# A three-layer graph network on one core: two neighbouring key columns stored side by side, and fetched with one gather for two

## The reference

```python
src = jnp.concatenate([edge_index[0], loops]); dst = jnp.concatenate([edge_index[1], loops])
deg = segment_sum(ones_like(dst), dst, num_segments=n)
dinv = where(deg > 0, rsqrt(deg), 0.0)
norm_edge = dinv[src] * dinv[dst]
for W, b in ((W1, b1), (W2, b2), (W3, b3)):
    h = h @ W
    h = relu(segment_sum(h[src] * norm_edge[:, None], dst) + b)
out = layernorm(x + h)
```

## Time and profile before

| | us |
|---|---|
| three runs | 2489.03, 2490.22, 2491.07 |
| median | 2490.22 |
| the profiled execution | 2488.2 |
| its span | 2486.4 |
| PE busy | 2271.8 (91%) |
| POOL busy | 1753.4 (71%) |
| DVE busy | 1027.0 (41%) |
| ACT busy | 521.7 (21%) |

### The profile page before, as it was taken

How to read it: one execution, slowest core, us unless ns; L and a number is a source line. 1 busy time by engine, 2 the same in 40 slices (tenths; PEclk the granted TensorE clock), 3 DMA queues, 4 the chain that set the end, 5 groups by cost and what they waited for, 6 DMA issues and landing times.

```text
span 2486.4 us, 42327 instructions
## 1 busy us (share of the span) xinstructions
PE 2271.8 (91%) x13351; PEld 1562.8 (63%) x13352; DVE 1027.0 (41%) x1307; ACT 521.7 (21%) x1322; POOL 1753.4 (71%) x1837
## 2 busy tenths in 40 slices
PE   6977799898999998999999999999988799999998
PEld 6855577676777773444444444444444688888887
DVE  8877333233333313444444444444422233333332
ACT  6611223222222312222222222222211000000000
POOL 5177777777777756777777777777776776767674
PEclk9788999999999999999999999999999899999999
DMA  6335666666666656888888888888887888888784
GB/s 215 119 118 184 222 203 206 201 198 205 192 209 190 208 170 204 253 272 268 267 264 264 263 267 264 264 268 258 275 260 236 261 257 249 252 248 255 245 247 140
DMA packets 231550, 568.24 MB, mean 229 GB/s; under 512 B 39868, under 2 KB 95795, under 8 KB 231475
## 3 DMA queue, kind: packets, MB, share of 16 engines
q0 software_dynamic: 126752, 399.62, 54.6%
q1 hardware_dynamic: 88371, 126.81, 14.5%
q10 hardware_dynamic: 16352, 40.77, 4.9%
HBM read 476.69 MB, written 90.36 MB: 228 GB/s over the span
## 4 chain that ended last, share of the span: by engine, by line
PE 55%; POOL 16%; issue 13%; DMA 7%; POOLq 4%; DVE 3%; ACT 0%; ACTq 0%; DVEq 0%; SPq 0%
POOL rows L671 16%; PE ps_acc L1511 9%; PE ps_h L1600 8%; PE ps_T L1600 7%; PE ps_o L1567 6%; DMA rows<-table,idx 5%; PE ps_d L1612 5%; PE ps_acc L1515 5%; PE ps_d L1515 4%; PE ps_h L1555 3%; PE ps_d L1511 3%; POOLq L680 3%; PE ps_d L1469 2%; DMA rows<-table_parts,idx 1%; PE ps_e L1588 1%
## 5 line engine op out<-in xcount | busy, mean ns | idle before, releaser
L671 POOL DMA_INDIRECT rows<-table,idx x912 | 870.0, 954 | 300.9 <-issue 264.7
L671 POOL DMA_INDIRECT rows<-table_parts,idx x884 | 837.1, 947 | 324.0 <-issue 268.2
L892 DVE SCALAR_TENSOR_TENSOR sel<-ps_e,firsts,dstT 128x1152 f32<-128x1152 f32 (+1 forms) x222 | 314.7, 1418 | 684.9 <-PE ps_acc L1511 253.9
L1515 PE MATMUL ps_acc<-rows,sel 128*128 128x512 f32 (+2 forms) x1122 | 489.8, 568 | 82.8 <-DMA rows<-table,idx 55.5
L1515 PE MATMUL ps_d<-rows,sel 128*128 128x512 f32 (+1 forms) x850 | 413.3, 616 | 41.3 <-DMA rows<-table,idx 41.2
L1511 PE MATMUL ps_acc<-rows,sel 128*128 128x256 bf16 (+1 forms) x2196 | 360.1, 280 | 50.5 <-DMA rows<-table_parts,idx 21.7
L1515 PEld LDWEIGHTS ps_acc<-rows,sel 128*128 128x128 f32 x1122 | 209.2, 202 | 250.0 <-issue 149.3
L1511 PEld LDWEIGHTS ps_acc<-rows,sel 128*128 128x128 bf16 x2196 | 217.9, 100 | 93.9 <-issue 37.8
L1515 PEld LDWEIGHTS ps_d<-rows,sel 128*128 128x128 f32 x850 | 152.8, 195 | 196.4 <-issue 119.2
L1567 PE MATMUL ps_o<-w,hT 128*128 128x512 f32 (+1 forms) x784 | 269.2, 486 | 1.2 <-ACT hT L1272 1.2
L1612 PE MATMUL ps_d<-parts,made_tiles 128*128 128x256 bf16 x1470 | 229.2, 272 | 0.5 <-issue 0.4
(11 more groups left out here) (190 smaller groups left out, 1902.8 us busy)
## 6 DMA issues: line engine op xcount, KB each, us to landing
built<-made_tiles SPq DMA_DIRECT2D x72, 384.0 KB
made_tiles<-built ACTq DMA_DIRECT2D x72, 384.0 KB
rows<-table,idx POOLq DMA_INDIRECT x912
rows<-table_parts,idx POOLq DMA_INDIRECT x884
table<-made SPq DMA_DIRECT2D x49, 256.0 KB
acc<-table SPq DMA_DIRECT2D x49, 256.0 KB
built<-made_tiles SPq DMA_DIRECT2D x24, 416.0 KB
made_tiles<-built ACTq DMA_DIRECT2D x24, 416.0 KB
```

The lines of the kernel that those rows point to most:

```text
L671: pool.indirect_dma_start(out=to, out_offset=None, in_=its[0:nodes, :], in_offset=bass.IndirectOffsetOnAxis(ap=idx[:, of, k:k + 1], axis=0 ...
L892: v.scalar_tensor_tensor(to[:, k:k + FRONT, :], numbers.unsqueeze(1).broadcast_to([P, FRONT, P]), firsts[:, bass.ds(t, 1)], dstT[:, bass.d ...
L1515: return mm(to[:, 0:w], sel[:, k, :], rows_of[phase][:, k, 0:w] if first is None else first, start=start, stop=stop)
```

## The change

In DRAM, `keys` becomes twice as wide: row c holds column c in its first 128 words, and column c + 1 in the second 128. SP stores the first halves as before, and the second halves with two further DMAs, both read from the same `raw_src`. Column c + 1 of partition q is partition q + 1 of the same block, so one store goes from partitions 1 to 127 of SBUF into the rows of q = 0 to 126; for q = 127 the neighbour is partition 0 of the next block, and that is the other store, 6 rows. The very last row's second half is not written. POOL waits for all three and fetches both columns of a chunk with one gather of 1 KB rows, six in place of twelve. `key_rows` keeps one row number for each chunk, and one of DVE's small instructions goes.

```diff
--- before.py
+++ after.py
@@ -118,7 +118,7 @@
 
 
 
-        keys = nc.dram_tensor("keys", (COLS, P), I32).ap()
+        keys = nc.dram_tensor("keys", (COLS, 2 * P), I32).ap()
         built = nc.dram_tensor("built", (DENSE * P, T * P), BF16).ap()
 
         raw = sb("raw", [P, 3, RA, P], I32)
@@ -207,7 +207,7 @@
         fill = sb("fill", [P, CHUNKS])
         fill_i = sb("fill_i", [P, CHUNKS], I32)
         over = sb("over", [P, CHUNKS])
-        key_rows = sb("key_rows", [P, 2, CHUNKS], I32)
+        key_rows = sb("key_rows", [P, CHUNKS], I32)
         bits = sb("bits", [P, len(SHIFTS), CHUNKS], I32)
         root = sb("root", [P, T])
         dinv = sb("dinv", [P, T])
@@ -467,7 +467,10 @@
             sp.wait_ge(place_out, 16)
             sp.dma_start(src_wide, places.rearrange("(a k) p -> a k p", a=1).broadcast_to([P, SLOTS, P])).then_inc(wide_in, 16)
             sp.wait_ge(keys_made, 1)
-            sp.dma_start(keys.rearrange("(a q) p -> q a p", q=P), raw_src).then_inc(keys_out, 16)
+            columns = keys.rearrange("(a q) p -> q a p", q=P)
+            sp.dma_start(columns[:, :, 0:P], raw_src).then_inc(keys_out, 16)
+            sp.dma_start(columns[0:P - 1, :, P:2 * P], raw_src[1:P, :, :]).then_inc(keys_out, 16)
+            sp.dma_start(columns[P - 1:P, 0:RA - 1, P:2 * P], raw_src[0:1, 1:RA, :]).then_inc(keys_out, 16)
             for g in range(XSTEPS):
                 by, nth_of = X_BY[g]
                 sp.wait_ge(x_scaled[by], nth_of)
@@ -701,14 +704,13 @@
                     else:
                         gather_if(need, phase, k, of, k, in_parts)
 
-            pool.wait_ge(keys_out, 16)
+            pool.wait_ge(keys_out, 16 * 3)
             pool.wait_ge(counts_in, 1)
             pool.wait_ge(key_rows_done, 1)
             for c in range(CHUNKS):
-                for side in range(2):
-                    pool.indirect_dma_start(
-                        out=kw[:, c, side * P:(side + 1) * P], out_offset=None, in_=keys[:, :],
-                        in_offset=bass.IndirectOffsetOnAxis(ap=key_rows[:, side, c:c + 1], axis=0)).then_inc(kw_in, 16)
+                pool.indirect_dma_start(
+                    out=kw[:, c, :], out_offset=None, in_=keys[:, :],
+                    in_offset=bass.IndirectOffsetOnAxis(ap=key_rows[:, c:c + 1], axis=0)).then_inc(kw_in, 16)
 
             def one_window():
                 for phase in range(3):
@@ -858,8 +860,7 @@
             v_.wait_ge(firsts_done, 1)
             step(v.tensor_copy(first_f[:, :, :], ps_acc[:, 0:2 * CHUNKS].rearrange("p (i c) -> p i c", i=2)))
             step(v.tensor_copy(first_i[:, :], first_f[:, 0, :]))
-            step(v.tensor_scalar(key_rows[:, 0, :], first_i[:, :], 7, None, ALU.arith_shift_right))
-            step(v.tensor_scalar(key_rows[:, 1, :], key_rows[:, 0, :], 1, None, ALU.add))
+            step(v.tensor_scalar(key_rows[:, :], first_i[:, :], 7, None, ALU.arith_shift_right))
             v_.wait_ge(next_in, 16 * 3)
             v.tensor_scalar(firsts[:, :], few[:, 0:T + 1], float(P), None, ALU.mult)
             step(v.tensor_copy(ends[:, :], raw_next[:, :, P - 2]))
@@ -1027,7 +1028,7 @@
 
             def shift_words():
 
-                v_.wait_ge(kw_in, 16 * 2 * CHUNKS)
+                v_.wait_ge(kw_in, 16 * CHUNKS)
                 for i, far in enumerate(SHIFTS):
                     n = P + far - 1
                     step(v.copy_predicated(kw[:, :, 0:n], bits[:, i, :].unsqueeze(2).broadcast_to([P, CHUNKS, n]),
```

## The result

| us | before | changed |
|---|---|---|
| median of 6 runs each | 2491.72 | 2505.29 |
| lowest to highest | 2489.03 to 2494.51 | 2501.90 to 2511.07 |
| the profiled execution | 2488.2 | 2504.32 |
| its span | 2486.4 | 2502.5 |
| mean granted clock of the profiled execution | 0.965 | 0.956 |

The ratio of the two is 1.0055, with a 95% interval of 1.0045 to 1.0065: by the medians the changed kernel is 13.6 us slower. The forecast was 2507.2, range 2500 to 2517.

What follows compares the result with a forecast made beforehand. POOL's full gather queue was taken to carry any delay of its first table gather to the end. The 127-row store on one engine delays the table, +17.0 us on 2488.2 gives 2505.2, plus 2.0 to the median: 2507.2, range 2500 to 2517.

Steps and rivals of the forecast that it cites:

- The store on one engine: Second keys' store, 127 x 7 rows: all rows go to one DMA engine of 16 and take 24.2 us.
- Its part of the table behind it: The slow engine's share of the seven table stores, 19.7 us, plus 1.4 for its part of the key gathers.
- Table landed at 145.7: `table0_out` complete at 145.7 us in place of 120.3, including 0.3 for the landing.
- The first table gather 1.8 us behind the landing, so +17.0: POOL's first table gather at 147.5 us, 17.0 later than 130.50.
- DVE +19.7: DVE's copy starts at 145.8 us, 19.7 late, and with it the splits, first sum and PE's opening of window 1.
- Rival C: DVE's splits set the pace of windows 1 to 3, 2.7 us not won back: 2509.9; within the forecast's 0.78.
- From then on everything is as late as POOL: After PE's waits for rows spend 2.7 us, everything downstream stays 17.0 us late.
- A: The 127-row store spreads over engines, table lands by 123.8, only 3.4 us of POOL's queue gained: 2486.8; chance 0.12.
- B: The lone engine is slower, 54 ns per 512-byte row, 48.5 us in place of 24.2: 2531.5; chance 0.04.
- D's second form: Table lands fully before the rest of the keys, so POOL's key gathers delay its table gathers: +23, 2513; chance 0.04.

Runs made afterwards that it cites:

- row counts: The kernel before, with eight extra stores of 128 to 112 partitions at its end, one after the other; 2565.13 us in one execution.
- padded kernel: The changed kernel with one more row in `keys`, so both halves are stored with 128 partitions; 2491.46 us, ratio 0.9995 to before.
- gathers-alone kernel: The kernel before without the six gathers of the column behind and without added stores; 2491.62 us, ratio 0.9996.
- slow store twice: The changed kernel with a second 127-row store in SP's queue, ahead of the table's stores; 2522.20 us, ratio 1.0125 to before.
- stores alone: The kernel before, twelve gathers kept, plus a 127-row and a 6-row store to DRAM that nobody reads; 2505.84 us, ratio 1.0059.
- slow store behind the table: The changed kernel with both added stores moved behind the table's seven stores in SP's queue; 2507.18 us, ratio 1.0063 to before.
- 126 rows and 1: The changed kernel with its 127-row store cut into one of 126 rows and one of 1; 2491.28 us, ratio 1.0004 to before.
- the one from POOL: The changed kernel with its two added stores issued by POOL on its own queue, not by SP; 2513.65 us, ratio 1.0082 to before.

## Why the prediction was right, and where its sizes were off

**The store on one engine** (forecast 24.2 us): it is. The share was 0.06 to 0.08 for 20 us, and the row counts show the rule at eight numbers. The term measured 21.5, since the lone engine moved 21.2 GB/s and not 18.8. I had taken the rate of before's 1.6 us of keys' store, where 16 engines were at work with a start and an end inside; the rate of the long full stretch, 20.6 in the prediction, was the nearer one.

**Its part of the table behind it** (19.7 + 1.4 = 21.1): about 18.8, from the end of the slow store near 120.9 to 139.7, where the last engine stops. The table's stores ran at 368 to 389 GB/s between 120 and 135 us, in before at 336. Nothing in the prediction could tell that; see the last section.

**Table landed at 145.7**: 140.0. The two terms above make 5.0 of the 5.7, 2.7 and 2.3, and are the ones furthest off. The other 0.7 is the first store's end, which was at 99.4 and not at 100.1. The landing came 0.3 behind the last data, as taken.

**The first table gather 1.8 us behind the landing, so +17.0**: 2.5 behind, and +12.0. DVE +19.7: +14.0. That DVE is later than POOL, here by 2.0 in place of 2.7, and that windows 1 to 3 spend it, was so. PE's waits in the changed kernel, 147 to 221 us, against the earlier trace rows (waits in all, times, longest):

```profile
PE ps_acc L1516 <- DMA rows<-table,idx: 7.5, 6, 2.3
```

PE waited 3.5 us less for rows, and the sums' lag fell from 14.1 to 12.7 in three windows, to what POOL's gathers have. Rival C falls with it.

**"From then on everything is as late as POOL"**: so up to window 12, and with one more step in it. At a delay of 12.1 the mechanism alone gives 2488.2 + 12.1 = 2500.3 for the profiled execution; it was 2504.3. The missing 4 us come at one place. Chain of waits before, and then in the changed kernel:

```profile
366.86 3.97 DMA rows<-table_parts,idx
...
370.87 1.16 PE ps_acc L1511 x9
372.03 1.79 PE ps_h L1555 x16
...
385.40 0.44 DVE acc L972
```

```profile
378.93 4.96 DMA rows<-table_parts,idx
...
383.94 2.10 PE ps_acc L1512 x9
386.04 3.41 PE ps_h L1556 x16
...
400.98 0.44 DVE acc L973
```

The same gather is issued 12.1 later and lands 13.1 later, and PE then needs 2.6 us more for the same 25 matmuls. Windows, before and then changed, over these matmuls (the granted clock is the number behind the busy times):

```profile
370.90:373.80 2.90, 2.90 (x27) 2.78 (x28) 1.63 (x2) 0.00 (x0) 2.29 (x3) 1.00 0.78 247
```

```profile
384.00:389.40 5.40, 5.40 (x26) 4.83 (x27) 3.21 (x2) 0.00 (x0) 4.18 (x5) 0.50 0.57 162
```

PE's row at the start of these matmuls, before and then changed (with the idle time ahead of it):

```profile
370.87 0.83 PE L1511 MATMUL ps_acc<-rows,sel 128*128 128x256 bf16 x6 [1.80 <-DMA rows<-table_parts,idx]
```

```profile
383.94 0.61 PE L1512 MATMUL ps_acc<-rows,sel 128*128 128x256 bf16 x2 [3.82 <-DMA rows<-table_parts,idx]
```

The granted clock was 0.50 here, the 1.2 GHz level, after PE had been idle for 3.8 us; before, PE had been idle for 1.8 us, and the clock was 1.00, 2.4 GHz. 1.0 for the gather and 2.6 for the clock are 3.6 of the 4.5 from 11.1 to 15.6; the other 0.9 is that the sum before had been 11.1 late and POOL's gathers 12.1. This is one gather in one execution.

The same step stands in traces that have nothing slow in them. In the padded kernel's the sums go from 3.2 ahead of before's to 0.8 behind in this window, and in the gathers-alone kernel's from 3.6 ahead to 1.2 behind; in the kernel with the slow store twice it is 2.4 us. PE of the padded kernel:

```profile
370.16 1.20 PE L1512 MATMUL ps_acc<-rows,sel 128*128 128x256 bf16 x9 [4.24 <-DMA rows<-table_parts,idx]
```

In these three PE had waited 4.24, 4.04 and 2.62 us for this gather, and the clock was 0.50 for a part of the 25 matmuls or for all. In three others there is no step: with the stores alone, with the slow store behind the table and with 126 rows and 1 PE had waited 2.29, 1.55 and 0.51 us, and the clock stayed at 1.00. Since kernels with and without the slow store are on both sides, I don't count the step as a cost of the change. Before's profiled execution is one in which this wait was short, and a fast one, 3.5 us under the median; why a gather lands sooner in one execution than in the next isn't shown. Medians against medians, +13.6 us, lie between POOL's 12.1 and the step's 15.6. The forecast of 2507.2 was thus helped by luck, with errors against each other. The delay was put 5 us too high, and a step of up to 4 us was left out. And the forecast stood on a median of before of 2490.2, which became 2491.72 with three more runs: the forecast time was 1.9 us off, the forecast change (17.0 against 13.6) 3.4.

**The rivals.** A (the store spreads) is refuted by the share; its side of the sum is not: without the slow store (padded, 126 and 1, the gathers alone) the three ratios are 0.9995, 1.0004 and 0.9996, which is no change. A had worked out 3.4 us of gain and called that too little to be told from none. B is refuted by 24.2 ns a row. D's second form is what the kernel with the slow store behind the table does, not this one: here the keys landed at 121.6, ahead of the table.

**Open:** where the 3.8 to 4.6 us go by which the first table gather is early in those three. In the padded kernel 2.2 of them are spent in the gaps of POOL's queue at 247.9 and 254.6; its chain of waits runs through DVE's splits from 232 to 244 us, so it is likely, though not tested, that DVE and PE set the pace there and not the gathers. In the gathers-alone kernel the lead fell from 4.4 to 2.4 by the 80th gather without such gaps, because the gathers' own rows took 2.0 us more in all, and in the 126-and-1 kernel 3.8 were left up to the 224th. The rest, up to 4 us, is too small for these runs to follow to the end.

The padded kernel and the one with 126 rows and 1 both mend the change, and neither can be told from the other or from before.

## What to carry to other kernels

Before a store is cut by one partition, work out the largest divisor up to 16 of its first dimension: 127 partitions ran 12.6 times as long as 128, and 126 plus 1 cost nothing that could be measured. (No load was tried here, only stores from SBUF to DRAM.) A DMA that is slow on one engine delays every later DMA that uses this engine, on its own queue and on others, so price it not by who waits for it but by who waits for anything issued behind it. And work taken out ahead of a wait is worth only what lies behind the wait's own end: the six gathers saved put POOL's first table gather 3.8 to 4.6 us ahead, and gave nothing that could be measured in the time.

## What else the runs showed of the hardware

- The issue of the DMA behind a slow store is held back: 20.56 us at L473, and 20.86, 20.50 and 22.58 in three other kernels, though the held one is only 6 rows. A long issue row names the store in front of it.
- The table's stores ran at two rates, with the same code and shapes: 336 to 339 GB/s in before, the padded kernel and the gathers-alone one, and mostly 384 to 389 in the changed kernel, the one with the slow store twice, the one with it behind the table, the 126-and-1 one, and at first in the one from POOL. The second group consists of those in which `keys` has exactly 896 rows of 256 words; with 897 rows it was 339. The stores-alone kernel had 338 to 373. What in it decides isn't settled; for the table's 6.42 MB it is 2.5 us.
- A gather took POOL 1.25 us (0.95 and 0.30 of idle) whether its rows had 512 bytes or 1 KB.
- A gather's row on POOL can be stretched beside one kind of DVE instruction. The key gathers at 116.57 of before (3.16 us) and 115.47 of the padded kernel (3.15) ran beside DVE's scaling of 128x2304 elements by a second operand, shown below for before. Those at 142.98 (3.28) and 146.56 (2.16) of the kernel with the store behind the table ran beside two other such TENSOR_TENSOR instructions of 128x2304 elements, 2.55 us each. DVE's selection matrices did not do it: the gathers at 120.03 and 121.28 of before ran beside them and took 0.94.

```profile
116.35 2.56 DVE L914 TENSOR_TENSOR rows<-rows,src_dinv 128x2304 f32<-128x2304 f32 x1
```
